# Edge network sweep of a graph kernel: expanded keys evicted ahead of head 3's norm, and VectorE's rectifier in eight pieces between the steps of the norm chain

## The chip, the cores and the metric

The kernel runs on one core of a Trainium2 chip. The metric is the device time of one execution in microseconds (us). Times before: 12400.16 us, median of 3 runs (12395.85 to 12402.57).

## What is computed

The reference is four graph layers on one graph of 6250 nodes and 206250 edges (100000 edges in both directions and a self loop for each node), 64 features a node, each layer followed by a residual sum and a layer norm: a normalised graph convolution (L0), an edge network with four heads (L1), a rectified message sum (L2), and an attention by cosine (L3). The change lies in L1 alone. What it computes for every edge and head h:

```python
alpha = concat([K_v[dst] * K_v[src], K_v[dst] * K_E], 1) * scale   # 128 values
gate  = sigmoid(layernorm(alpha) * ln_g + ln_b)
m     = (concat([V_v[src], V_E], 1) @ Wu[h] + bu[h]) * gate
m     = leaky(layernorm(m @ Wm[h] + bm[h]) * mln_g + mln_b)        # leaky: max(v, 0.01 v)
heads.append(segment_sum(m, dst, N))
```

Here `K_v = x @ Kv2v[h]`, `K_E = edge_feature @ Ke2v[h]`, and the V's alike; `K_v[dst]` are the keys that the kernel expands from nodes to edges.

## The kernel before, in words

The program has stages one behind the other: degrees, a dense adjacency matrix in HBM and the keys of the edges (to about 4160 us), the edge network's sweep, called sweep1 (4166 to 10470 us), then L2 and L3. The edges are sorted by destination and cut into tiles of 128 edges; four tiles (G = 4) make a group, and sweep1 runs over NG = 404 groups. Each engine has its own instruction stream, all written out by hand with semaphores; each runs an iteration i of a software pipeline in which the stages of several groups meet. The first 8 iterations and the last ones are written out, the rest run in a hardware loop of four iterations.

In iteration i, in this order on each engine:

- **TensorE**: `turn_x` (4 transposes of group i's features, L1233); `turn(0)`, `m_u(0)`, `turn(1)`, `m_u(1)` (`turn(h)`: 4 transposes of head h's normed alpha of group i-1, L1240; `m_u(h)`: two matmuls, L1248); `o_pair(0)` (L1253, L1259); `expand(i+1, 0)` (L1214: the one-hot of destinations times the nodes' keys, tiles 0 and 1, into PSUM bank 7); `turn(2)`, `m_u(2)`; `expand(i+1, 1)` (tiles 2 and 3 into the same bank 7, so it waits at L1212 for `q_out`, that ScalarE has taken the first half out); `turn(3)`, `m_u(3)`; `clear_sums` (L1266), `sums(0)` (L1274, waits for `msg_ready`), `o_pair(1)`, `sums(1)`. `turn(h)` waits for head h's norm (`normed`, L1237).
- **ScalarE**: `sigmoid(0)`, `sigmoid(1)` (L1020); the copy of the turned features (L1036); `norm(i-1, 2)` (four activations, L1014); `take_sums` (L1004, L1005); `norm(i-1, 3)`; `take_q(i+1, 0)` (L986: bank 7 to SBUF; it waits for `q_done`, the matmuls of `expand`, and sets `q_out`); `sigmoid(2)`; `take_o(0)` (L1027, L1028); `take_q(i+1, 1)`; `sigmoid(3)`; `norm(i, 0)`, `norm(i, 1)`, which wait for VectorE's chain; `take_o(1)`.
- **VectorE**: `stats` of tiles 0 and 1 (8 bn_stats, L716); `gate_m(0)` (L722, waits for `sigmoid(0)`); `stats` of tiles 2 and 3; `gate_m(1)`; the rectifier `leaky` of group i-4's messages y (L742, one instruction over 1024 columns, behind a wait for `y_affine`); the **chain**, 15 small steps (L761 to L788) that make the inverse roots for the alpha norm of group i and the output norm of group i-3, with a wait for the step before (`settle`, L751) between dependent ones; among them a reduction over 1040 columns (L764); `gate_m(2)`, `gate_m(3)` (waits for `sigmoid(3)`); `product` (L699); `turn_hot` (L706); and y = o times its inverse root (L800, sets `chain2`).
- **GpSimd**: four gathers (L1434), then `affine` of the y that L800 left (L1486, L1489, sets `y_affine`); it waits at L1486 for `chain2`.
- **SyncE** only issues the loads: kept keys, edge features, the nodes' keys near a group, destination rows, one-hots.

Of the kernel before, what the change touches and what calls it, by code (L numbers as in the profile page):

```python
# [20 lines left out]
ALU = mybir.AluOpType  # L21
ACT = mybir.ActivationFunctionType
AX = mybir.AxisListType.X
# [13 lines left out]
NG = T // G  # L37
# [54 lines left out]
def after(eng, semaphore, value):  # L92

    if not isinstance(value, int) or value > 0:
        eng.wait_ge(semaphore, value)


def gnn(nc, a, out):
    ctx = ExitStack()
    with ctx:  # L100
# [157 lines left out]
        o_sq = [view(G * H * (D + 1), [G * H, D + 1]) for _ in range(2)]  # L258
        y = [view(G * H * D, [G * H, D]) for _ in range(2)]
        st = view(G * H * 6, [G * H, 6])  # L260
        var, u = (view(2 * G * H, [2 * G * H]) for _ in range(2))
# [89 lines left out]
        chain1 = sem("chain1")  # L351
# [8 lines left out]
        o_taken = sem("o_taken")  # L360
# [3 lines left out]
        y_affine = sem("y_affine")  # L364
        msg_ready = sem("msg_ready")
        CH = 15
# [74 lines left out]
        def _(dve):  # L441
            V = nc.vector
# [84 lines left out]
            for c in range(EDGES):  # L527
                count(base_f, RUNS, c, whole_runs)
                if (c + 1) % PART == 0:
                    dve.wait_ge(dve_step, vcount[0])  # L530
                    part = slice(c + 1 - PART, c + 1)
# [25 lines left out]
            for j in range(1, S):  # L557
                own = col_f[:, j * R:(j + 1) * R]
# [22 lines left out]
            for i in range(3):  # L581
                part = bm_part[i][:, :].rearrange("p (h d) -> p h d", h=H)
# [72 lines left out]
            for half in range(2):  # L655
                dve.wait_ge(pe_batch, pe_number["fold0", half])
                own = acc[0:D, 0, half * HALF:(half + 1) * HALF].rearrange("p (i n) -> p i n", n=CH_N)
# [31 lines left out]
            Q = G * H  # L689
# [19 lines left out]
            def sweep1(i, k, s, inside):  # L709

                now = [inside or 0 <= i - lag < NG for lag in range(5)]
                z, odd = s % 2, (s + 1) % 2
# [24 lines left out]
                    stats(3)  # L737
                if now[1]:
                    gate_m(1)
                if now[4]:  # L740
                    dve.wait_ge(y_affine, 2 * (i - 3))
                    V.scalar_tensor_tensor(y[z], y[z], 0.01, y[z], ALU.mult, ALU.max).then_inc(msg_ready, 1)  # L742


                n = [0]

                def small_step(ins):
                    ins.then_inc(chain1, 1)
                    n[0] += 1

                def settle():  # L751
                    dve.wait_ge(chain1, i * CH + n[0])

                if now[0]:
                    dve.wait_ge(stats1, Q * (i + 1))
                if now[3]:
                    dve.wait_ge(o_taken, 2 * (i - 2))
                root = rstd[z]
                if now[2]:
                    dve.wait_ge(normed, Q * (i - 1))  # L760
                small_step(V.tensor_tensor(d2, st[:, :, 1], st[:, :, 4], ALU.subtract))  # L761
                small_step(V.tensor_tensor(sm, st[:, :, 1], st[:, :, 4], ALU.add))
                small_step(V.scalar_tensor_tensor(m2, st[:, :, 2], P * EPS1, st[:, :, 5], ALU.add, ALU.add))
                small_step(V.tensor_reduce(var[:, Q:2 * Q], o_sq[odd], AX, ALU.add))  # L764
                settle()

                small_step(V.scalar_tensor_tensor(d2, d2, P / 4.0, d2, ALU.mult, ALU.mult))
                settle()
                small_step(V.tensor_tensor(var[:, 0:Q], d2, m2, ALU.add))
                settle()  # L770
                small_step(V.tensor_scalar(root.bitcast(I32), var.bitcast(I32), -0.5, MAGIC, ALU.mult, ALU.add))

                settle()
                small_step(V.scalar_tensor_tensor(u, root, 1.0, root, ALU.mult, ALU.mult))
                settle()
                small_step(V.tensor_tensor(u, u, var, ALU.mult))
                settle()
                small_step(V.scalar_tensor_tensor(u, u, -10.0 / 3.0, u, ALU.add, ALU.mult))
                settle()
                small_step(V.scalar_tensor_tensor(root, u, 5.0, root, ALU.add, ALU.mult))  # L780
                settle()
                small_step(V.scalar_tensor_tensor(u, root, -0.5 * 0.375 ** 3 * P ** 0.5, root, ALU.mult, ALU.mult))
                settle()
                small_step(V.tensor_tensor(u, u, var, ALU.mult))
                settle()
                small_step(V.scalar_tensor_tensor(root, u, 1.5 * 0.375 * P ** 0.5, root, ALU.add, ALU.mult))
                settle()
# [151 lines left out]
        def _(act):  # L939
# [42 lines left out]
            def take_q(g, j):  # L982

                act.wait_ge(q_done, 2 * g + j + 1)
                after(act, products, g)
                A.activation(q[:, 2 * j:2 * j + 2, :].rearrange("p t n -> p (t n)"), psum[:, 7, :],  # L986
                             ACT.Copy).then_inc(q_out, 1)

            def sweep1(i, k, s, inside):
# [8 lines left out]
                def take_sums():  # L998

                    act.wait_ge(sums1, 2 * (i - 4))  # L1000
                    after(act, added1, 3 * (i - 5))
                    for half in range(2):
                        own = acc[:, half, bass.ds(held[s], 1)]
                        A.activation(own, psum[:, half, 0:1], ACT.Identity, bias=own).then_inc(added1, 1)  # L1004
                    A.activation(acc[:, :, 1:NW][:, :, bass.ds(held[s], G * WIN - 1)], psum[:, 0:2, 1:G * WIN],  # L1005
                                 ACT.Copy).then_inc(added1, 1)
# [32 lines left out]
                    norm(i - 1, (s + 3) % U, odd, 2)  # L1039
                if now[5]:  # L1040
                    take_sums()
                if now[1]:
                    norm(i - 1, (s + 3) % U, odd, 3)
                if inside or i + 1 < NG:
                    take_q(i + 1, 0)
                if now[1]:
                    sigmoid(2)
                if now[2]:
# [649 lines left out]
```

## Time and profile before

The profiled execution took 12403.94 us; its span from the first to the last instruction is 12402.1 us.

| engine | busy, us | share of the span |
|---|---|---|
| TensorE matmul | 9426.5 | 76% |
| VectorE | 8554.8 | 69% |
| ScalarE | 6685.0 | 54% |
| GpSimd | 6548.5 | 53% |

These shares are averages over stages with different limits. Sweep1 takes half of the span, from about 4160 to 10470 us, and only there do all engines run at once; the change touches only that stretch. So the views to read are those of windows inside it. The whole-span chain of waits is spread over five stages and says little about one of them.

### The profile page before, as it was taken

Reading aid. Unit: us, or ns where it says so; the run is one execution under the profiler, and the core shown is the slowest. Engines: PE = TensorE matmul, PEld = TensorE weight load, DVE = VectorE, ACT = ScalarE, POOL = GpSimd, SP = SyncE. Lnnn points to the kernel's source line nnn. Section 1 sums busy time; section 2 is a strip of 40 time slices with the busy share of each in tenths; the row PEclk is TensorE's granted clock in tenths of the full one; section 3 lists DMA queues with packets and bytes.
Section 4 is the critical chain, followed back from the end, with each engine's and each line's share of the span. In section 5 each row is a group of like instructions: output and inputs, shape, how many; then the busy total and the mean of one; then the engine's idle time right before and its main releaser. Section 6 shows DMA issues by size and latency. Waiting matters only on the chain.

```text
span 12402.1 us, 195341 instructions
## 1 busy us (share of the span) xinstructions
PE 9426.5 (76%) x48422; PEld 6119.9 (49%) x48423; DVE 8554.8 (69%) x19173; ACT 6685.0 (54%) x13488; POOL 6548.5 (53%) x4199
## 2 busy tenths in 40 slices
PE   1344444444446799999999999999999997769996
PEld 1233333333322566666666666666666665333222
DVE  4233333333311799999999999999999998047896
ACT  0111111111100488888888888888888886026442
POOL 1588888888840366666666666666666664000000
PEclk9999999999999799999999999999999998989997
DMA  9866666666678455555555555555555553869663
GB/s 412 257 163 150 152 150 151 150 152 152 149 234 337 153 152 152 152 152 152 152 152 152 152 152 152 152 152 152 152 152 152 152 152 109 355 255 358 206 218 118
DMA packets 1446102, 2253.42 MB, mean 182 GB/s; under 512 B 352561, under 2 KB 981762, under 8 KB 1432131
## 3 DMA queue, kind: packets, MB, share of 16 engines
q1 hardware_dynamic: 1129144, 1975.67, 48.0%
q0 software_dynamic: 312672, 272.36, 13.6%
q10 hardware_dynamic: 4144, 3.51, 0.1%
q8 instruction: 88, 1.44, 0.0%
q14 instruction: 54, 0.44, 0.0%
HBM read 1758.01 MB, written 492.97 MB: 181 GB/s over the span
## 4 chain that ended last, share of the span: by engine, by line
PE 42%; POOL 15%; ACT 15%; issue 12%; DMA 8%; DVE 3%; SPq 3%; ACTq 1%; DVEq 0%; POOLq 0%; PEldq 0%
POOL adj L1473 14%; ACT arena L1014 8%; PE psum L1274 6%; PE psum L1259 6%; PE psum L1248 5%; PE psum L1345 5%; DMA arena<-adj 5%; PE psum L1240 4%; PE psum L1214 4%; SPq L1520 3%; ACT acc L1005 3%; DMA adj<-put_val,put_idx 3%; PE psum L1390 2%; PE psum L1266 2%; ACT arena L986 2%
## 5 line engine op out<-in xcount | busy, mean ns | idle before, releaser
L1473 POOL DMA_INDIRECT adj<-put_val,put_idx x1616 | 2640.7, 1634 | 842.6 <-issue 477.2
L1155 PE MATMUL psum<-ke,arena 64*128 64x256 f32 x3232 | 1451.8, 640 | 1883.2 <-DMA arena<-in_edge_t 1883.2
L1014 ACT ACTIVATE arena<-arena 128x128 f32<-128x128 f32 x6464 | 2624.5, 501 | 19.1 <-DVE arena L788 9.1
L1434 POOL DMA_INDIRECT arena<-table,idx_blk x1616 | 1938.1, 1199 | 451.3 <-issue 409.3
L1155 PEld LDWEIGHTS psum<-ke,arena 64*128 64x128 f32 x3232 | 1041.6, 330 | 2292.9 <-issue 2025.9
L971 ACT ACTIVATE arena<-psum 128x512 f32<-128x512 f32 x808 | 482.5, 597 | 2921.5 <-PE psum L1155 2611.7
L1486 POOL TENSOR_TENSOR arena<-arena,mg 128x1024 f32<-128x1024 f32 x404 | 953.6, 2360 | 1973.7 <-DVE arena L800 1973.7
L1248 PE MATMUL psum<-arena,wvu 128*128 128x512 f32 x3232 | 1655.3, 594 | 0.0
L1259 PE MATMUL psum<-wm,arena 128*128 128x64 f32 x12928 | 1616.3, 278 | 0.0
L1259 PEld LDWEIGHTS psum<-wm,arena 128*128 128x128 f32 x12928 | 1505.4, 192 | 183.3 <-issue 181.5
L1020 ACT ACTIVATE arena<-psum,cols 128x512 f32<-128x512 f32 x1616 | 1263.2, 782 | 495.0 <-PE psum L1240 494.6
L614 DVE TENSOR_TENSOR arena<-arena 128x1024 f32<-128x1024 f32 x202 | 247.8, 1227 | 1723.2 <-DMA arena<-key_lin 1723.2
L716 DVE BATCH_NORM_STATS2 arena<-arena 128x6 f32<-128x128 f32 x6464 | 1320.9, 277 | 0.0
L722 DVE SCALAR_TENSOR_TENSOR arena<-psum,cols,arena 128x512 f32<-128x512 f32 x1616 | 1199.4, 746 | 24.5 <-PE psum L1248 4.5
L1214 PE MATMUL psum<-arena 128*128 128x256 f32 x3232 | 897.5, 400 | 364.4 <-ACT arena L986 315.5
L1240 PE MATMUL psum<-ident,arena 128*128 128x128 f32 x6464 | 970.8, 273 | 5.6 <-ACT arena L1014 4.4
L1489 POOL TENSOR_TENSOR arena<-arena,mb 128x1024 f32<-128x1024 f32 x404 | 952.6, 2358 | 31.7
L1240 PEld LDWEIGHTS psum<-ident,arena 128*128 128x128 f32 x6464 | 795.8, 141 | 303.7 <-issue 212.4
L1274 PE MATMUL psum<-arena 128*128 128x128 f32 x6464 | 921.2, 286 | 6.5 <-DVE arena L742 6.5
L699 DVE TENSOR_TENSOR arena<-arena 128x2048 f32<-128x2048 f32 x404 | 921.4, 2281 | 5.8 <-ACT arena L986 5.8
L1214 PEld LDWEIGHTS psum<-arena 128*128 128x128 f32 x3232 | 551.9, 191 | 742.0 <-ACT arena L986 631.8
L1274 PEld LDWEIGHTS psum<-arena 128*128 128x128 f32 x6464 | 789.1, 192 | 179.6 <-issue 179.6
(218 smaller groups left out, 12787.6 us busy)
## 6 DMA issues: line engine op xcount, KB each, us to landing
arena<-adj SPq DMA_DIRECT2D x192, 1568.0 KB, 12.5
arena<-adj SPq DMA_DIRECT2D x336, 896.0 KB, 4.7
kept_keys<-arena SPq DMA_DIRECT2D x404, 512.0 KB
arena<-kept_keys SPq DMA_DIRECT2D x404, 512.0 KB
arena<-table1q SPq DMA_DIRECT2D x1616, 128.0 KB
adj<-arena SPq DMA_DIRECT2D x98, 1568.0 KB
arena<-in_edge_t SPq DMA_DIRECT2D x808, 128.0 KB
kept_hot<-arena SPq DMA_DIRECT2D x404, 256.0 KB
```

Of the source, the lines that this page charges most:

```text
L716: V.bn_stats(st[:, t * H + h, :], halves(pair[s][:, :, D:PAIR])[:, t, :, h * D:(h + 1) * D]).then_inc(stats1, 1)
L722: V.scalar_tensor_tensor(gm[odd][:, h, :, :].rearrange("p t n -> p (t n)"), psum[:, 4 + h % 2, :], cols[:, 0, h:h + 1], gate[:, h % 2, :], ...
L1014: A.activation(to, at_, ACT.Identity, bias=shift[z][:, n:n + 1], scale=rstd[z][:, n:n + 1]).then_inc(normed, 1)
L1020: A.activation(gate[:, h % 2, :], psum[:, 2 + h % 2, :], ACT.Sigmoid, bias=cols[:, 2, h:h + 1], scale=cols[:, 1, h:h + 1]).then_inc(gated, 1)
L1155: last = M.matmul(psum[:, 2 + 2 * z + j, t * H * D:(t + 1) * H * D], edge0[z][:, 2 * j + t, :], ke[D:P, :], start=True, stop=True)
L1214: last = M.matmul(psum[:, 7, t * H * D:(t + 1) * H * D], hot_t[:, 2 * j + t, :], near[at_z][:, 2 * j + t, :], start=True, stop=True)
L1240: last = M.transpose(psum[:, 2 + h % 2, t * P:(t + 1) * P], normal[h % 2][:, t, :], ident[:, :])
L1248: M.matmul(psum[:, 4 + h % 2, :], wvu[:, h, :], xt[prev].rearrange("p t n -> p (t n)"), start=True, stop=True).then_inc(m_done, 1)
L1259: last = M.matmul(psum[:, 6, at_ + h * D:at_ + (h + 1) * D], gm[z][:, h, 2 * j + t, :], wm[:, h, :], start=False, stop=t * H + h == 2 * H - 1)
L1274: last = M.matmul(psum[:, half, bass.ds(held[G * s + t], WIN)], y[z][:, t * H + 2 * half:t * H + 2 * half + 2, :].rearrange("p h d -> p (h ...
L1434: K.indirect_dma_start(out=dst[:, t, :], out_offset=None, in_=table, in_offset=bass.IndirectOffsetOnAxis(ap=idx[:, t:t + 1], axis=0)).then ...
L1473: K.indirect_dma_start(out=adj, out_offset=bass.IndirectOffsetOnAxis(ap=put_idx[s][:, j:j + 1], axis=0), in_=put_val[s][:, j:j + 1], in_of ...
```

## The change

Two edits, both inside sweep1.

On ScalarE `take_q(i + 1, 0)` moves in front of `norm(i - 1, 3)`; the order of everything else stays.

On VectorE the rectifier L742, one instruction over 16 x 64 = 1024 columns, becomes eight instructions over 2 x 64 = 128 columns each (`leaky(0)` to `leaky(7)`). They no longer stand ahead of the chain: one stands behind each of eight steps of it, from `var[:, 0:Q]` (L769) to the second `u * var` (L784), ahead of the wait for that step. The wait for `y_affine` goes with `leaky(0)`, and `msg_ready` is set by `leaky(7)`. The reduction L764 moves from the fourth to the fifth place of the chain, behind the squared difference, with the wait for `o_taken` now just ahead of it.

```diff
--- before.py
+++ after.py
@@ -737,12 +737,19 @@
                     stats(3)
                 if now[1]:
                     gate_m(1)
-                if now[4]:
-                    dve.wait_ge(y_affine, 2 * (i - 3))
-                    V.scalar_tensor_tensor(y[z], y[z], 0.01, y[z], ALU.mult, ALU.max).then_inc(msg_ready, 1)
 
 
                 n = [0]
+                piece = Q // 8
+
+                def leaky(part):
+                    if now[4]:
+                        if part == 0:
+                            dve.wait_ge(y_affine, 2 * (i - 3))
+                        own = y[z][:, part * piece:(part + 1) * piece, :]
+                        done = V.scalar_tensor_tensor(own, own, 0.01, own, ALU.mult, ALU.max)
+                        if part == 7:
+                            done.then_inc(msg_ready, 1)
 
                 def small_step(ins):
                     ins.then_inc(chain1, 1)
@@ -753,35 +760,45 @@
 
                 if now[0]:
                     dve.wait_ge(stats1, Q * (i + 1))
-                if now[3]:
-                    dve.wait_ge(o_taken, 2 * (i - 2))
+                else:
+                    after(dve, chain1, i * CH)
                 root = rstd[z]
                 if now[2]:
                     dve.wait_ge(normed, Q * (i - 1))
                 small_step(V.tensor_tensor(d2, st[:, :, 1], st[:, :, 4], ALU.subtract))
                 small_step(V.tensor_tensor(sm, st[:, :, 1], st[:, :, 4], ALU.add))
                 small_step(V.scalar_tensor_tensor(m2, st[:, :, 2], P * EPS1, st[:, :, 5], ALU.add, ALU.add))
+                settle()
+
+                small_step(V.scalar_tensor_tensor(d2, d2, P / 4.0, d2, ALU.mult, ALU.mult))
+                if now[3]:
+                    dve.wait_ge(o_taken, 2 * (i - 2))
                 small_step(V.tensor_reduce(var[:, Q:2 * Q], o_sq[odd], AX, ALU.add))
                 settle()
-
-                small_step(V.scalar_tensor_tensor(d2, d2, P / 4.0, d2, ALU.mult, ALU.mult))
-                settle()
                 small_step(V.tensor_tensor(var[:, 0:Q], d2, m2, ALU.add))
+                leaky(0)
                 settle()
                 small_step(V.tensor_scalar(root.bitcast(I32), var.bitcast(I32), -0.5, MAGIC, ALU.mult, ALU.add))
+                leaky(1)
 
                 settle()
                 small_step(V.scalar_tensor_tensor(u, root, 1.0, root, ALU.mult, ALU.mult))
+                leaky(2)
                 settle()
                 small_step(V.tensor_tensor(u, u, var, ALU.mult))
+                leaky(3)
                 settle()
                 small_step(V.scalar_tensor_tensor(u, u, -10.0 / 3.0, u, ALU.add, ALU.mult))
+                leaky(4)
                 settle()
                 small_step(V.scalar_tensor_tensor(root, u, 5.0, root, ALU.add, ALU.mult))
+                leaky(5)
                 settle()
                 small_step(V.scalar_tensor_tensor(u, root, -0.5 * 0.375 ** 3 * P ** 0.5, root, ALU.mult, ALU.mult))
+                leaky(6)
                 settle()
                 small_step(V.tensor_tensor(u, u, var, ALU.mult))
+                leaky(7)
                 settle()
                 small_step(V.scalar_tensor_tensor(root, u, 1.5 * 0.375 * P ** 0.5, root, ALU.add, ALU.mult))
                 settle()
@@ -1039,10 +1056,10 @@
                     norm(i - 1, (s + 3) % U, odd, 2)
                 if now[5]:
                     take_sums()
+                if inside or i + 1 < NG:
+                    take_q(i + 1, 0)
                 if now[1]:
                     norm(i - 1, (s + 3) % U, odd, 3)
-                if inside or i + 1 < NG:
-                    take_q(i + 1, 0)
                 if now[1]:
                     sigmoid(2)
                 if now[2]:
```

## Rows read from the trace of the kernel before

**Rows 1.** Windows: us, busy of each engine, clock, DMA share, GB/s; sweep1.

```profile
4700.00:10500.00 5800.00, 5489.14 (x32666) 3926.01 (x32664) 5444.11 (x14463) 5092.96 (x11116) 3533.25 (x2305) 1.00 0.54 150
```

**Rows 2.** Waits, 4800 to 10400: who waited for whom, us, times, longest.

```profile
PE psum L1214 <- ACT arena L986: 282.5, 360, 0.9
...
DVE arena L742 <- POOL arena L1489: 151.2, 360, 0.5
```

**Rows 3.** Timeline, one iteration: TensorE; start, us, instructions, idle before.

```profile
7508.36 1.02 PE L1248 MATMUL psum<-arena,wvu 128*128 128x512 f32 x2
...
7509.23 0.60 PE L1240 MATMUL psum<-ident,arena 128*128 128x128 f32 x4
...
7512.77 1.08 PE L1214 MATMUL psum<-arena 128*128 128x256 f32 x4
...
7514.12 1.02 PE L1248 MATMUL psum<-arena,wvu 128*128 128x512 f32 x2
...
7515.93 1.13 PE L1214 MATMUL psum<-arena 128*128 128x256 f32 x4 [0.78 <-ACT arena L986]
...
7516.90 0.60 PE L1240 MATMUL psum<-ident,arena 128*128 128x128 f32 x4
...
7518.82 1.16 PE L1274 MATMUL psum<-arena 128*128 128x128 f32 x8
...
7524.74 0.60 PE L1240 MATMUL psum<-ident,arena 128*128 128x128 f32 x4
```

**Rows 4.** The same timeline: ScalarE, from sigmoid(1) to sigmoid(3).

```profile
7509.86 0.78 ACT L1020 ACTIVATE arena<-psum,cols 128x512 f32<-128x512 f32 x1 [0.44 <-PE psum L1240]
...
7513.75 1.65 ACT L1014 ACTIVATE arena<-arena 128x128 f32<-128x128 f32 x4
...
7515.29 0.59 ACT L986 ACTIVATE arena<-psum 128x512 f32<-128x512 f32 x1
...
7517.86 0.79 ACT L1020 ACTIVATE arena<-psum,cols 128x512 f32<-128x512 f32 x1
```

**Rows 5.** The same timeline: VectorE and GpSimd around the rectifier and chain.

```profile
7507.83 1.64 DVE L716 BATCH_NORM_STATS2 arena<-arena 128x6 f32<-128x128 f32 x8
...
7512.83 1.23 DVE L742 SCALAR_TENSOR_TENSOR arena<-arena 128x1024 f32<-128x1024 f32 x1 [0.35 <-POOL arena L1489]
...
7513.97 0.18 DVE L761 TENSOR_TENSOR arena<-arena 128x16 f32<-128x16 f32 x1
...
7515.24 0.96 POOL L1434 DMA_INDIRECT arena<-table,idx_blk  x1 [0.30 <-issue]
...
7515.73 0.17 DVE L769 TENSOR_TENSOR arena<-arena 128x16 f32<-128x16 f32 x1
...
7515.94 0.25 DVE L771 TENSOR_SCALAR arena<-arena 128x32 int32<-128x32 int32 x1
...
7517.98 1.53 DVE L722 SCALAR_TENSOR_TENSOR arena<-psum,cols,arena 128x512 f32<-128x512 f32 x2
```

**Rows 6.** Timeline of VectorE, early in the sweep.

```profile
4347.35 1.23 DVE L742 SCALAR_TENSOR_TENSOR arena<-arena 128x1024 f32<-128x1024 f32 x1 [0.51 <-POOL arena L1489]
...
4362.76 1.23 DVE L742 SCALAR_TENSOR_TENSOR arena<-arena 128x1024 f32<-128x1024 f32 x1 [0.50 <-POOL arena L1489]
```

**Rows 7.** Timeline of TensorE behind the last product: turn(3) without expand.

```profile
10418.66 0.66 PE L1240 MATMUL psum<-ident,arena 128*128 128x128 f32 x4 [1.22 <-ACT arena L1014]
```

**Rows 8.** Timeline of ScalarE there: norm(3).

```profile
10416.96 1.65 ACT L1014 ACTIVATE arena<-arena 128x128 f32<-128x128 f32 x4
```

**Rows 9.** Timeline of VectorE, end of the sweep.

```profile
10441.01 1.23 DVE L742 SCALAR_TENSOR_TENSOR arena<-arena 128x1024 f32<-128x1024 f32 x1 [4.90 <-POOL arena L1489]
```

**Rows 10.** DMA queues, 4300 to 10380: instruction packets, MB, share.

```profile
q14 instruction: 5, 0.04, 0.0%
q8 instruction: 2, 0.03, 0.0%
```

**Rows 11.** DMA issues of the whole run: KB each, us to landing.

```profile
arena<-kept_hot SPq DMA_DIRECT2D x404, 256.0 KB, 3.4
```

## The prediction

> **What bounds the kernel now.** I read three views of sweep1. First the windows: from 4700 to 10500 us TensorE is busy 5489 of 5800 us and VectorE 5444 [rows 1], at a granted clock of 1.00 (the 2.4 GHz level). Two engines at 94% mean that shares can't say which one sets the pace. Next the waits: TensorE waits at L1214 for ScalarE's L986 in all of 360 iterations, 282.5 us together, and VectorE at L742 for GpSimd's L1489, 151.2 us [rows 2]. These are the only stalls of the two that come every time. Then the timeline of one iteration: turn(1) starts at 7509.23 and again at 7524.74 [rows 3], 15.51 later (15.52 over longer stretches, which I use). Times below are in us after 7500.
>
> The loop that closes at 15.52 runs through two engines. ScalarE starts sigmoid(1) at 9.86 as turn(1) ends, and works without a gap through norm(2), take_sums and norm(3) (from 13.75) to take_q, 15.29 to 15.88 [rows 4]; only then, at 15.93, may TensorE start expand(i+1, 1), after 0.78 of idling [rows 3]. The rest, from there to the next turn(1), is TensorE's own work. The bank was full at 12.77 + 1.08 = 13.85 [rows 3], so take_q comes 1.44 late, behind a norm that TensorE doesn't need yet.
>
> A second loop is almost as long. Early in the sweep two rectifiers stand 4362.76 - 4347.35 = 15.41 apart, each behind a wait of 0.51 for GpSimd [rows 6]: L800, then affine, then L742, then all of VectorE's iteration. VectorE's own work is thus 15.41 - 0.51 = 14.90. So moving take_q alone could give only about 15.52 - 15.41 = 0.11 a group; it takes both edits to go further.
>
> **Part 1, take_q ahead of norm(3).** Nothing is added; two pieces trade places. ScalarE is free at 13.75, but the bank is full at 13.85 and a release takes about 0.04, so take_q starts at 13.89 (0.14 of new waiting) and is done at 14.48. It held the engine for 15.77 - 15.29 = 0.48 before norm(3)'s successor started (ScalarE has no gap there), so norm(3) starts at 14.37 instead of 13.75. TensorE: m_u(2) starts at 14.12 [rows 3]; an m_u that waits for nothing is followed after 9.23 - 8.36 = 0.87 [rows 3], so expand(i+1, 1) starts at 14.99, not 15.93. Its wait is gone. What is late next is turn(3), which needs norm(3). It follows expand after 16.90 - 15.93 = 0.97 [rows 3], so it could start at 15.96; behind the last product, where no expand stands between, turn(3) started at 10418.66 after a norm(3) begun at 10416.96 [rows 7, 8], 1.70 later. So 14.37 + 1.70 = 16.07 instead of 16.90: **0.83 saved**, and a remnant of 0.11 waiting at turn(3). The new period of this loop is 14.69. With norm(3) wholly hidden it would be 14.58, TensorE's own work; that is the floor. Behind turn(3) nothing else depends on the order: sigmoid(2) starts 0.14 later, as does sigmoid(3) (now 17.86, then 18.00 to 18.79) [rows 4]. The SyncE load and GpSimd gather that wait for `normed` fetch for groups two iterations ahead, so 0.6 later is covered; bare, it would cost those 0.6.
>
> **Part 2, the rectifier.** Removed from VectorE: L742, which holds it for 13.97 - 12.83 = 1.14 [rows 5], and the 0.51 wait ahead of it. The chain's first steps, with the 1.23 of the reduction, run meanwhile: L761 to L769 took 15.73 - 13.97 = 1.76 [rows 5], so leaky(0) asks for `y_affine` over 1.7 later than L742 would, and the wait is gone. If it came back, all chain steps, both gate_m and the product would queue behind it. Added: eight pieces between dependent steps. From L769 to gate_m(2) ten starts take 17.98 - 15.73 = 2.25, 0.225 each [rows 5]; that is latency, since the work is far smaller. What a piece holds: eight bn_stats of 128 columns take 1.64, at most 0.205 each, and L742 takes 1.14 for 1024 columns [rows 5], which makes 1.04 ns a column and 0.07 fixed. A 32-column step then holds 0.105, a 128-column piece 0.205, together **0.31 from step to step**, since the step's result has arrived while the piece runs. Growth of the chain: 8 x (0.31 - 0.225) = 0.68. VectorE's work: 14.90 - 1.14 + 0.68 = 14.44, under 14.69 by 0.25. Moving the reduction only reorders; its steps sum to the same 1.76, or one settle (0.1) less. Late next on VectorE is gate_m(3), which waits for sigmoid(3) at 18.79; VectorE idles its 0.25 there. The messages: leaky(7) ends about 0.7 ahead of gate_m(2), near 17.5, and sums(0) wants them at 18.82 - 0.83 = 17.99 [rows 3]. That cover is 0.4 thick.
>
> No row shows a piece between two dependent steps. Lower bound: fully inside the latency, s = 0.225, growth 0 and no effect on the time, as TensorE leads. Upper bound: nothing overlaps. L742 lasts 1.23 and holds 1.14, so a piece lasts 0.205 + 0.09 = 0.29; a 16-column step lasts 0.17 [rows 5], one of 32 columns 0.19, and the next starts 0.225 - 0.19 = 0.035 after its end: 0.19 + 0.035 + 0.29 + 0.035 = 0.55. I take 0.31, because bn_stats and L742 both overlap their neighbours [rows 5]. In general VectorE's work is 11.96 + 8s: it passes 14.69 at s = 0.341 and 15.52 at s = 0.445. GpSimd's gathers run beside the chain; L771 takes 0.25 where it ends with a gather [rows 5] against about 0.19 for its neighbours, so up to 0.06 x 4 = 0.24 a group might be added, just the slack.
>
> The Trainium skill speaks against this part ("VectorE: DVE Perf Modes", section "The DRAIN you can't avoid"): the next instruction does not start until the pipe is empty. The trace disagrees: at 0.29 each, eight bn_stats would take 2.3, and they take 1.64 [rows 5]. By that rule s would be near 0.55, and the change would lose; it is rival C.
>
> **The sum.** 404 groups less the first few, which follow other waits: 400 x 0.83 = 332. In the last three iterations VectorE waits 4.90 for GpSimd [rows 9]; there the chain's first 1.76 now runs under the wait while the pieces lengthen what follows by 0.68 and the last message waits longer, so some 4 in all. 12403.94 - 336 = 12068 for the profiled execution; the median of the runs is 3.8 lower, so **12064**. The bounds of this case: period 14.58 gives 400 x 0.94 = 376 and 12024; 14.80, with gather contention or 0.1 more at turn(3), gives 288 and 12112.
>
> **Rivals.**
> - **B, VectorE leads.** A satisfied wait lets the next step in only when the piece has ended: s = 0.105 + 0.29 + 0.035 = 0.43, work 15.40, gain 0.12 x 400 = 48, 12350; milder forms lie between this and the forecast. For: dependent steps start 0.035 after the end of the one before. Against: gate_m and stats follow each other with overlap though waits stand between them.
> - **C, slower.** The pieces and steps don't overlap at all, s = 0.55: work 16.36, 0.84 x 400 = 336 lost, 12736. It decides from s = 0.445. Against it are the 1.64 of rows 5.
> - **D, instructions fetched again.** VectorE's loop grows by 7 instructions an iteration, 28 in its body of four. Now 7 packets of instructions move in 6080 us [rows 10], so every loop stays resident. If this one no longer did, each of 98 passes would wait for a load, at most about the 3.4 of a 256 KB one-hot [rows 11], less the slack of 4 x 0.25: 98 x 2.4 = 235 given back, 12299; with a 1 us fetch, nothing. The Trainium skill ("Runtime: NRT & Kernel Launch", section "Instruction fetch mechanics") says that a branch to a page outside the two held stalls; no row of before shows such a stall.
> - **E, no effect**, if the release of bank 7 didn't gate TensorE: the wait would reappear in full at turn(3), giving 12400. Against: turn(3) has the whole expand (0.97) as cover.
>
> **How the numbers follow.** Forecast 70%; B 12%, D 8%, C 6%, E 4%. Forecast's own range is 12024 to 12112. To leave out no more than 2 in 10 the range takes in the milder halves of B and D: 12015 to 12270. A measurement of this kernel can tell about 0.2%, 25 us. Faster: forecast, D, and B nearly whole, 0.89; same 0.05; slower 0.06.
>
> **What would show it.** In the changed profile: the idle at L1214 behind ScalarE gone and about 0.1 at turn(3) in its place; turn(1) every 14.7; no wait for `y_affine`; chain steps with a piece 0.31 apart; a wait of 0.2 to 0.3 at gate_m(3) for sigmoid(3). Steps 0.35 or more apart with no idle left on VectorE mean B or C; a gap of over 1 us every fourth iteration with hundreds of instruction packets means D; idle at sums(0) would mean that the later messages bind.

## The result, and the profile of the changed kernel

The changed kernel takes 12111.44 us (median of 4, 12107.74 to 12115.86) against 12399.56 us before (median of 4, 12395.85 to 12402.57): ratio 0.9766, 95% interval [0.9755, 0.9778]. That is 288 us less where 336 were forecast, 48 us above the forecast of 12064, inside the stated range (12015 to 12270) and 0.6 us under the upper end of the forecast's own 12024 to 12112. The profiled execution took 12110.71 us, its span is 12108.9 us; against the profiled execution of before it saves 293.2 us.

In the changed file lines from the rectifier on stand 7 to 17 lower. On VectorE the pieces are L750, the chain's first steps L768, L769, L770, L773, the reduction L776, then L778 to L805, `product` L699, y's scaling L817; ScalarE has `take_q` L1003, `take_sums` L1021 and L1022, `norm` L1031, `sigmoid` L1037; TensorE `expand` L1231, `turn` L1257, `m_u` L1265, `clear_sums` L1283, `sums` L1291; GpSimd the gathers L1451 and the affine L1503, L1506.

The windows view of sweep1 (core time, busy us and instructions of TensorE, its weight loads, VectorE, ScalarE and GpSimd, clock, DMA share, GB/s) and the waits from 4800 to 10100 (us in total, times, longest):

```profile
4700.00:10200.00 5500.00, 5461.81 (x32538) 3911.58 (x32537) 5419.31 (x16989) 5062.55 (x11069) 3321.26 (x2293) 1.00 0.53 157
```

```profile
PEld psum L1257 <- ACT arena L1031: 164.8, 359, 0.5
...
PEld psum L1231 <- ACT arena L1003: 85.3, 357, 0.2
```

TensorE is now busy 5462 of 5500 us, 99.3% where it was 94.6% [rows 1]. Both stalls of [rows 2] are gone: `expand` no longer idles behind ScalarE's `take_q` (the 0.2 that is left is a weight load's), and no line of VectorE waits for GpSimd. In their place is a wait at `turn(3)` for norm(3) in each of 359 iterations, 0.46 for the weight load; TensorE's matmuls themselves lose little by it, as the timeline shows.

The timeline of one iteration (start, duration, engine and line, count, idle before):

```profile
7502.23 2.36 POOL L1506 TENSOR_TENSOR arena<-arena,mb 128x1024 f32<-128x1024 f32 x1
...
7503.68 1.08 PE L1231 MATMUL psum<-arena 128*128 128x256 f32 x4
...
7504.03 0.60 DVE L768 TENSOR_TENSOR arena<-arena 128x16 f32<-128x16 f32 x1
...
7504.56 0.17 DVE L769 TENSOR_TENSOR arena<-arena 128x16 f32<-128x16 f32 x1
...
7504.80 0.60 ACT L1003 ACTIVATE arena<-psum 128x512 f32<-128x512 f32 x1
...
7505.29 1.63 ACT L1031 ACTIVATE arena<-arena 128x128 f32<-128x128 f32 x4
...
7506.22 0.17 DVE L778 TENSOR_TENSOR arena<-arena 128x16 f32<-128x16 f32 x1
...
7506.80 0.18 DVE L785 SCALAR_TENSOR_TENSOR arena<-arena 128x32 f32<-128x32 f32 x1
...
7506.90 0.28 DVE L750 SCALAR_TENSOR_TENSOR arena<-arena 128x128 f32<-128x128 f32 x1
...
7506.98 0.66 PE L1257 MATMUL psum<-ident,arena 128*128 128x128 f32 x4
...
7507.11 0.18 DVE L788 TENSOR_TENSOR arena<-arena 128x32 f32<-128x32 f32 x1
...
7507.48 1.02 PE L1265 MATMUL psum<-arena,wvu 128*128 128x512 f32 x2
...
7508.45 0.28 DVE L750 SCALAR_TENSOR_TENSOR arena<-arena 128x128 f32<-128x128 f32 x1
...
7508.97 1.16 PE L1291 MATMUL psum<-arena 128*128 128x128 f32 x8
...
7509.04 1.54 DVE L722 SCALAR_TENSOR_TENSOR arena<-psum,cols,arena 128x512 f32<-128x512 f32 x2
...
7514.89 0.38 PE L1257 MATMUL psum<-ident,arena 128*128 128x128 f32 x2
```

turn(1) stands at 7500.14 and again at 7514.89, 14.75 later (15.51 in [rows 3]; the last line shows two of its four matmuls because the window ends there). Over 4100 us in the middle of the sweep one product follows the other after 14.784 in the mean, 15.524 before; I call this the period.

### The profile page after: what moved, and what is told of

It is laid out like the page before. It is cut to its first block, busy times and chain, and to the rows that moved or that the text cites. A ratio compares the mean times of both kernels' runs of the same rounds, so it can differ in the third digit from the quotient of the medians.

```text
span 12108.9 us, 197973 instructions
## 1 busy us (share of the span) xinstructions
PE 9428.1 (78%) x48422; PEld 6126.0 (51%) x48423; DVE 8560.2 (71%) x22001; ACT 6675.6 (55%) x13488; POOL 6342.6 (52%) x4199
## 4 chain that ended last, share of the span: by engine, by line
PE 54%; POOL 14%; DMA 10%; issue 9%; ACT 5%; SPq 3%; DVE 3%; DVEq 0%; ACTq 0%; POOLq 0%; another core or an unknown queue 0%; PEldq 0%
POOL adj L1490 14%; PE psum L1276 13%; PE psum L1265 8%; PE psum L1291 7%; PE psum L1362 5%; PE psum L1257 5%; DMA arena<-adj 5%; ACT arena L1031 5%; DMA adj<-put_val,put_idx 4%; PE psum L1231 3%; SPq L1537 3%; PE psum L1407 3%; PE psum L1270 2%; PE psum L1283 2%; PE psum L1250 1%
## 5 line engine op out<-in xcount | busy, mean ns | idle before, releaser
L1031 ACT ACTIVATE arena<-arena 128x128 f32<-128x128 f32 x6464 | 2613.6, 492 | 2.3 <-DVE arena L797 1.5
L1451 POOL DMA_INDIRECT arena<-table,idx_blk x1616 | 1726.6, 1068 | 456.5 <-issue 411.1
L1503 POOL TENSOR_TENSOR arena<-arena,mg 128x1024 f32<-128x1024 f32 x404 | 952.5, 2358 | 1889.3 <-DVE arena L817 1889.3
L1265 PE MATMUL psum<-arena,wvu 128*128 128x512 f32 x3232 | 1655.6, 594 | 0.0
L1037 ACT ACTIVATE arena<-psum,cols 128x512 f32<-128x512 f32 x1616 | 1254.8, 777 | 418.7 <-PE psum L1257 418.4
L1257 PE MATMUL psum<-ident,arena 128*128 128x128 f32 x6464 | 993.8, 276 | 28.9 <-ACT arena L1031 5.4
L1257 PEld LDWEIGHTS psum<-ident,arena 128*128 128x128 f32 x6464 | 763.4, 141 | 447.6 <-issue 212.4
L1506 POOL TENSOR_TENSOR arena<-arena,mb 128x1024 f32<-128x1024 f32 x404 | 952.5, 2358 | 31.7
L1291 PE MATMUL psum<-arena 128*128 128x128 f32 x6464 | 920.8, 286 | 8.5 <-DVE arena L750 6.3
L699 DVE TENSOR_TENSOR arena<-arena 128x2048 f32<-128x2048 f32 x404 | 921.7, 2281 | 5.8 <-issue 5.8
L750 DVE SCALAR_TENSOR_TENSOR arena<-arena 128x128 f32<-128x128 f32 x3232 | 914.7, 283 | 0.0
L1231 PE MATMUL psum<-arena 128*128 128x256 f32 x3232 | 856.0, 387 | 49.7 <-issue 47.3
L1291 PEld LDWEIGHTS psum<-arena 128*128 128x128 f32 x6464 | 790.0, 193 | 191.7 <-issue 191.7
```

The source lines that it names most:

```text
L1031: A.activation(to, at_, ACT.Identity, bias=shift[z][:, n:n + 1], scale=rstd[z][:, n:n + 1]).then_inc(normed, 1)
L1037: A.activation(gate[:, h % 2, :], psum[:, 2 + h % 2, :], ACT.Sigmoid, bias=cols[:, 2, h:h + 1], scale=cols[:, 1, h:h + 1]).then_inc(gated, 1)
L1231: last = M.matmul(psum[:, 7, t * H * D:(t + 1) * H * D], hot_t[:, 2 * j + t, :], near[at_z][:, 2 * j + t, :], start=True, stop=True)
L1257: last = M.transpose(psum[:, 2 + h % 2, t * P:(t + 1) * P], normal[h % 2][:, t, :], ident[:, :])
L1265: M.matmul(psum[:, 4 + h % 2, :], wvu[:, h, :], xt[prev].rearrange("p t n -> p (t n)"), start=True, stop=True).then_inc(m_done, 1)
L1291: last = M.matmul(psum[:, half, bass.ds(held[G * s + t], WIN)], y[z][:, t * H + 2 * half:t * H + 2 * half + 2, :].rearrange("p h d -> p (h ...
```

## The experiments

Each ratio is against the kernel before on the same chip, whose median there was 12409.46 (e1 to e4), 12400.53 (e5 to e7), 12402.54 (e8, e9) and 12404.72 us (e10).

### e1: ScalarE's swap alone

```diff
                 if now[5]:
                     take_sums()
+                if inside or i + 1 < NG:
+                    take_q(i + 1, 0)
                 if now[1]:
                     norm(i - 1, (s + 3) % U, odd, 3)
-                if inside or i + 1 < NG:
-                    take_q(i + 1, 0)
```

> Only the ScalarE edit; VectorE as before. Theory (two loops): the TensorE/ScalarE loop falls to 14.75 us, but the VectorE/GpSimd loop of 15.40 (own work 14.90 and a wait of 0.5 for the affine) then leads, so the period is 15.40, the gain 0.12 x 395 = 47, time 12350 (ratio 0.996), and the wait of 0.5 at the rectifier comes in every group. Rival (the two edits add up, each on its own stall): 0.77 a group at once, 12100, ratio 0.976.

12362.61 us, ratio 0.9964 [0.995, 0.9978], period 15.416. The waits view, 5000 to 9000:

```profile
DVE arena L742 <- POOL arena L1489: 132.1, 260, 0.5
...
PE psum L1240 <- ACT arena L1014: 106.8, 260, 0.4
```

VectorE now waits 0.51 (132.1 / 260) for GpSimd in every group where it was 0.42 (151.2 / 360, [rows 2]): with the TensorE loop shortened, the loop through L742 and the affine sets the pace, at the 15.41 that the prediction read out of [rows 6]. TensorE's surplus shows as idle at turn(3).

### e2: the pieces alone

The changed kernel with ScalarE's old order.

> Only the VectorE edit; ScalarE evicts the expanded keys behind head 3's norm as before. Theory: the TensorE/ScalarE loop stays at 15.52, time 12400 within 10 (ratio 1.000). Rival (the rectifier was what held the sweep): up to 0.7 a group gained, 12120, ratio 0.978.

12416.72 us, ratio 1.0004 [0.9995, 1.0014], period 15.540. TensorE:

```profile
7511.63 1.13 PE L1231 MATMUL psum<-arena 128*128 128x256 f32 x4 [0.80 <-issue]
```

The 0.78 of idle ahead of `expand(i+1, 1)` [rows 3] stands there undisturbed, as 0.80. e1 and e2 are worth 47 us and nothing, both together 288: two loops of nearly one length, each of which hides the other's gain.

### e3: the rectifier moved, but whole

```diff
-                        own = y[z][:, part * piece:(part + 1) * piece, :]
+                        own = y[z]
...
-                        if part == 7:
-                            done.then_inc(msg_ready, 1)
+                        done.then_inc(msg_ready, 1)
```

and only `leaky(0)` is called.

> The changed kernel with the rectifier as one instruction of 1024 columns in the place of the first piece. Theory: a step that a piece stands behind takes 0.30 instead of 0.225, so eight pieces cost 0.6 a group and one whole instruction 1.0; VectorE's loop goes from about 14.65 to 15.05 and leads; period 15.05, 0.27 x 395 = 107 slower than the changed kernel, 12218 (ratio to before 0.985). Rival (the pieces hide nothing, their fixed costs eat the gain): 12111 or less, ratio 0.977 or less.

12233.7 us, ratio 0.9857 [0.9841, 0.9873], period 15.10. VectorE and ScalarE:

```profile
7511.28 1.22 DVE L750 SCALAR_TENSOR_TENSOR arena<-arena 128x1024 f32<-128x1024 f32 x1
...
7512.42 0.17 DVE L780 TENSOR_SCALAR arena<-arena 128x32 int32<-128x32 int32 x1
...
7512.62 0.19 DVE L783 SCALAR_TENSOR_TENSOR arena<-arena 128x32 f32<-128x32 f32 x1
...
7512.85 0.19 DVE L785 TENSOR_TENSOR arena<-arena 128x32 f32<-128x32 f32 x1
...
7514.50 2.81 ACT L1023 ACTIVATE arena<-arena 128x128 f32<-128x128 f32 x7 [1.42 <-DVE arena L793]
```

The bare steps stand 0.20 to 0.23 apart, of which the step itself holds the engine for 0.105 by the prediction's estimate, and ScalarE waits 1.42 for the chain's end. So the swap and the move give 176 us, and the cutting into pieces the rest of the 288, about 112; by the periods it is 0.32 a group (15.10 less 14.78).

### e4: GpSimd's second affine instruction left out

The profile of the changed kernel has a row that the prediction did not foresee: the chain's first step, 16 columns, lasts 0.60 (L768 above; 0.599 in the median of 408), where its like lasts 0.18, and it ends 0.04 after GpSimd's L1506 (7504.63 and 7502.23 + 2.36 = 7504.59; L769 starts at 7504.56). e4 takes away what may hold it.

```diff
-                                ALU.mult).then_inc(y_affine, 1)
-                pool.wait_ge(y_affine, 2 * g + 1)
-                K.tensor_tensor(y4, y4, mb[:, :].unsqueeze(1).to_broadcast([P, G, H * D]),
-                                ALU.add).then_inc(y_affine, 1)
+                                ALU.mult).then_inc(y_affine, 2)
```

> The changed kernel without GpSimd's second affine instruction: the addition of the output norm's offset (mln_b) is left out, so messages lack it. Theory (a two-input VectorE instruction is held while a GpSimd tensor instruction runs): the chain's first step, now 0.60, lasts 0.18, since GpSimd is done 2.4 earlier; the messages come 0.4 earlier and sums(0) no longer waits; period 14.78 to 14.75, about 12098 (ratio 0.9757). Rival (the step is slow because it reads what bn_stats has just written): it stays at 0.60, time 12111.

12227.6 us, ratio 0.9852 [0.9836, 0.9868]: by the ratios 0.0086, or 107 us, slower than the changed kernel. The hold is gone, and something else has come:

```profile
7507.72 1.08 PE L1231 MATMUL psum<-arena 128*128 128x256 f32 x4
7507.75 0.95 POOL L1451 DMA_INDIRECT arena<-table,idx_blk  x1 [0.30 <-issue]
...
7508.12 0.18 DVE L768 TENSOR_TENSOR arena<-arena 128x16 f32<-128x16 f32 x1
...
7509.26 0.60 ACT L1003 ACTIVATE arena<-psum 128x512 f32<-128x512 f32 x1 [0.44 <-PE psum L1231]
...
7511.44 0.66 PE L1257 MATMUL psum<-ident,arena 128*128 128x128 f32 x4 [0.40 <-ACT arena L1031]
```

`take_q` starts 1.54 after `expand` began instead of 1.12 (7503.68 to 7504.80 above), and turn(3) 0.40 late behind it. In 203 of 332 iterations it was 1.48 or more; nearly all others kept 1.12. The theory was right on the hold (L768 is back at 0.18) and wrong on the time. GpSimd is also free 2.36 earlier, so its gathers start earlier, and e8 asks about those.

### e5: two probes on VectorE

Two more instructions of 16 columns on a scratch tile, one of one input in SBUF, one of two.

```diff
+                V.tensor_scalar(small[:, 16:32], small[:, 0:16], 2.0, None, ALU.mult)
...
+                V.tensor_tensor(small[:, 32:48], small[:, 0:16], small[:, 0:16], ALU.add)
```

> The changed kernel with two extra VectorE instructions of 16 columns an iteration on a scratch tile: one with a single SBUF input behind the first eight bn_stats, one with two SBUF inputs behind the second eight. Both stand in the time of GpSimd's affine. Theory (held while GpSimd runs): the first lasts about 0.17, the second about 1.2, to the end of the second affine instruction; the chain's first step then lasts 0.18, since the lock is over; VectorE's loop grows by gate_m(1)'s 0.65 and 0.1: period 15.4, about 12350 (ratio 0.996). Rival (the chain's first step was slow because of the bn_stats results): both probes 0.17, the first step stays at 0.60, period 14.85 to 15.0, about 12140 to 12200.

12509.61 us, ratio 1.0085 [1.0069, 1.01], period 15.79.

```profile
7506.40 2.36 POOL L1505 TENSOR_TENSOR arena<-arena,mg 128x1024 f32<-128x1024 f32 x1 [8.51 <-DVE arena L819]
...
7507.79 1.00 DVE L732 TENSOR_SCALAR small<-small 128x16 f32<-128x16 f32 x1
...
7508.83 2.36 POOL L1508 TENSOR_TENSOR arena<-arena,mb 128x1024 f32<-128x1024 f32 x1
...
7510.92 0.31 DVE L739 TENSOR_TENSOR small<-small 128x16 f32<-128x16 f32 x1
...
7511.81 0.17 DVE L770 TENSOR_TENSOR arena<-arena 128x16 f32<-128x16 f32 x1
```

The two-input probe ends at 7511.23, where L1508 ends (7511.19), and the chain's first step behind it, in the old place, is back at 0.17: held is whichever such instruction comes first, until GpSimd's instruction ends. But the one-input probe was held as well, 1.00 instead of 0.17, to 0.03 behind the end of L1505 (7508.76); I had expected it to pass freely. That is not what missed 12350: the second probe has the less left to stand, 0.31 where I expected 1.2, and the chain begins after L1508 either way. Of 259 intervals between products 227 are 15.4 to 15.5, as expected; the other 32 are 18.1 to 18.2, and in them TensorE's steps behind sums(0) last nearly twice as long. The windows view shows a granted clock of 0.97 from 5000 to 9000, where the changed kernel has 1.00. In 404 groups these breaks make some 130 of the 160 us. bn_stats and `gate_m`, which reads one operand in PSUM, run beside the affine at their usual 0.205 and 0.73.

### e6: y's scaling ahead of the product

`product` and `turn_hot` move behind the scaling of y, so that the affine starts some 2.8 us earlier, beside these two, which both have two inputs in SBUF.

```diff
-                if inside or i + 1 < NG:
-                    product(i + 1, k + (s + 1) // U, (s + 1) % U)
-                if inside or i + 2 < NG:
-                    turn_hot(i + 2)
...
+                if inside or i + 1 < NG:
+                    product(i + 1, k + (s + 1) // U, (s + 1) % U)
+                if inside or i + 2 < NG:
+                    turn_hot(i + 2)
```

> The changed kernel with the scaling of y (which releases GpSimd's affine) ahead of the product and turn_hot, two instructions with two SBUF inputs. Theory (held while GpSimd runs): they now fall into the 4.8 us of the affine and one waits for the other; period between 16 and 19, 12600 to 13800 (ratio 1.02 to 1.11). Rival (no such hold; the earlier affine only takes a wait away): period 14.75, 12098, ratio 0.976.

13148.56 us, ratio 1.0604 [1.0588, 1.062], period 17.39.

```profile
7515.26 2.29 DVE L699 TENSOR_TENSOR arena<-arena 128x2048 f32<-128x2048 f32 x1
...
7515.43 4.34 POOL L1503 TENSOR_TENSOR arena<-arena,mg 128x1024 f32<-128x1024 f32 x1 [6.01 <-DVE arena L813]
...
7517.47 2.85 DVE L706 TENSOR_TENSOR arena<-arena,rel 128x512 f32<-128x512 int32 x1
...
7519.84 2.69 POOL L1506 TENSOR_TENSOR arena<-arena,mb 128x1024 f32<-128x1024 f32 x1
```

Here is the same collision in both directions. The product was there first and keeps its 2.29; GpSimd's multiplication stands still meanwhile and takes 4.34 in place of 2.36. `turn_hot` then comes second and takes 2.85 in place of 0.68: it ends at 7520.32, 0.55 behind L1503 (7519.77). Whoever comes second stands until the first is nearly done and then takes its own whole time. The start of that time, counted back from its end, lies 0.12 to 0.15 before the recorded end of the first in every case here: `turn_hot` 7520.32 - 0.68 = 7519.64 against 7519.77, L768 7504.63 - 0.18 = 7504.45 against 7504.59, GpSimd's L1503 behind the product 7519.77 - 2.36 = 7517.41 against 7517.55.

The period is not the price of the hold alone: 118 of 235 intervals are 16.4, the rest 17.9 to 19.7, and the windows view shows a granted clock of 0.89 from 5000 to 9100.

### e7: the sums taken behind the eviction

With the hold known, I asked which engine leads in the changed kernel: TensorE behind norm(3), or VectorE.

```diff
-                if now[5]:
-                    take_sums()
-                if inside or i + 1 < NG:
-                    take_q(i + 1, 0)
                 if now[1]:
                     norm(i - 1, (s + 3) % U, odd, 3)
+                if inside or i + 1 < NG:
+                    take_q(i + 1, 0)
+                if now[5]:
+                    take_sums()
```

> The changed kernel with ScalarE's order norm(2), norm(3), take_q(0), take_sums: the norm in front again, the eviction of the sums moved behind instead. Theory: norm(3) starts at 12.56 of the iteration, take_q at 14.1, both in time for TensorE (14.99 and 15.96), so the remnant of 0.11 at turn(3) and the slow start of 0.06 go; the TensorE loop falls to 14.58 and VectorE's loop of about 14.63 to 14.65 leads, with sums(0) waiting for the last piece: 0.14 x 395 = 55 faster than the changed kernel, 12055 (ratio 0.972). Rival (VectorE already sets the pace of the changed kernel at 14.78): no change, 12111, ratio 0.977.

12083.65 us, ratio 0.9745 [0.9732, 0.9758], period 14.706: some 27 us less than the changed kernel, half of the 55 that I expected, and the fastest of the kernels that leave nothing out. Its waits, 5000 to 9000:

```profile
PEld psum L1276 <- DVE arena L722: 29.9, 132, 0.2
PE psum L1291 <- DVE arena L750: 28.4, 129, 0.3
```

No wait at turn(3) is left; TensorE waits for VectorE now, at sums(0) and o_pair(1). TensorE's loop no longer leads, VectorE's does, at 14.71 and not at the 14.63 to 14.65 that I had put, with L768 held as before (0.595 in the median). VectorE's busy share from 5000 to 9000 is 99.3%.

### e8: e4 with the gathers held back

```diff
+                after(pool, chain1, (g - 2) * CH + 4)
                 gather(pair[s][:, :, 0:ROW1], table1, idx, kv_in[s])
```

> As e4_no_second_affine (GpSimd's second affine instruction, the addition of mln_b, is left out), and GpSimd waits ahead of each group's gathers until VectorE's chain has done its fourth step, so that the gathers start where they start in the changed kernel (0.07 before the eviction) and not 2.3 earlier. The question is why the first eviction of the expanded keys started 0.44 after its release in two iterations of three of e4. Theory: the earlier gathers delay it. Then the eviction starts 0.04 after the expansion's end again, the period falls from the mean of 15.0 to 14.75, and the kernel takes 12,080 to 12,110 us. Rival: it hangs on VectorE's own earlier lead (its first step 0.42 shorter, which this kernel leaves as it is in e4). Then the eviction is late again and the time is 12,228 within 15 us.

12104.74 us, ratio 0.9759 [0.9743, 0.9775], period 14.765.

```profile
7504.72 1.08 PE L1231 MATMUL psum<-arena 128*128 128x256 f32 x4
...
7505.12 0.18 DVE L768 TENSOR_TENSOR arena<-arena 128x16 f32<-128x16 f32 x1
...
7505.84 0.60 ACT L1003 ACTIVATE arena<-psum 128x512 f32<-128x512 f32 x1
...
7506.50 0.98 POOL L1451 DMA_INDIRECT arena<-table,idx_blk  x1 [3.19 <-DVE arena L773]
...
7508.02 0.66 PE L1257 MATMUL psum<-ident,arena 128*128 128x128 f32 x4
```

The eviction is back at 1.12 behind `expand`, and so is the time (0.0093 between the ratios, 115 us). So the loss in e4 came with the earlier gathers, not with VectorE's lead. How a gather delays it is not shown: in e4 slow and fast iterations can have their gathers at the same offsets from `expand` to 0.01 us (-1.26, 0.03, 1.29, 2.54 with 1.54; -1.26, 0.03, 1.28, 2.54 with 1.12). The gathers did not come back to their old place, though: they start 0.66 behind the eviction (7506.50) and not 0.07 ahead of it, 3.0 later than in e4. With that reserve e8 against the changed kernel also prices the hold where TensorE leads: 14.784 less 14.765, 0.02 a group; the 7 us between the times are within their noise.

### e9 and e10: e7 without the hold

e9 is e7 with e4's edit, e10 is e9 with e8's.

> The order of e7_sums_behind on ScalarE (heads 2 and 3 normalised in one go, then the eviction, then the sums) with GpSimd's second affine instruction (the addition of mln_b) left out. In e7_sums_behind VectorE's loop set the period: all its instructions stand end to end and its first step is held 0.42. Theory: with nothing of GpSimd's left to hold that step VectorE's loop falls to 14.3 and TensorE's own floor of 14.58 to 14.65 is what is left: 0.05 to 0.12 less than the 14.70 of e7_sums_behind in 400 groups, 12,035 to 12,065 us. Rival: the late eviction of e4 comes back (its release is not in what this order changes); it then holds the second expansion and the time is 12,150 to 12,230.

12260.34 us, ratio 0.9879 [0.9863, 0.9896]. Both expectations missed. (The late eviction did come back in part: it starts 1.41 or more behind `expand` in 84 of 270 iterations, where 1.33 is usual in this order.) Of 272 intervals between products in mid-sweep 62 are 14.2 to 14.4 and 121 are 14.5 to 14.9, but 17 are 15.4 to 15.7, 48 are 16.1 to 16.5 and 24 about 18. In the last kind:

```profile
5152.15 1.15 PE L1291 MATMUL psum<-arena 128*128 128x128 f32 x8 [1.24 <-DVE arena L750]
...
5153.55 3.62 PE L1276 MATMUL psum<-wm,arena 128*128 128x64 f32 x16
```

TensorE idles 1.24 ahead of sums(0), and the next `o_pair` takes 3.62 in place of 2.00, at a granted clock of 0.52 from 5153.5 to 5157.2: the 1.2 GHz level. Such a break costs 3.3 in one group.

> As e9_sums_behind_no_second (order norm(2), norm(3), eviction, sums on ScalarE; GpSimd's second affine instruction, the addition of mln_b, is left out), and the gathers wait for VectorE's fourth chain step as in e8_gathers_held. e9 ran in groups of 14.2 to 14.8 broken by groups of 16.1 and 18.0, in which TensorE waited up to 1.24 ahead of the sums and then ran at half clock for some microseconds. Theory: those breaks come from the earlier gathers, as the late eviction of e4 did. Then they are gone, the period is TensorE's own floor of 14.57 to 14.65 (VectorE's loop is 14.25 without the held step), and the kernel takes 12,035 to 12,065 us. Rival: they come from the order with a shorter VectorE loop itself, whatever the gathers do. Then the groups of 16 and 18 stay and the time is 12,200 to 12,270 us.

12004.55 us, ratio 0.9677 [0.966, 0.9693], period 14.508, not one interval over 14.65 in mid-sweep. The breaks are gone as expected; the time is 30 us below the range that I gave. The window 5000 to 9000, and two lines of TensorE:

```profile
5000.00:9000.00 4000.00, 3998.94 (x24264) 2933.64 (x24263) 3942.54 (x12679) 3749.49 (x8271) 1796.35 (x1449) 1.00 0.54 163
```

```profile
7510.70 1.03 PE L1231 MATMUL psum<-arena 128*128 128x256 f32 x4
7511.56 0.60 PE L1257 MATMUL psum<-ident,arena 128*128 128x128 f32 x4
```

TensorE is busy 3998.9 of 4000: this is its own work with next to nothing waited for, 14.51 a group (sums(0) still starts 0.04 late in the mean, so 14.47 is the floor). The prediction's floor of 14.58 was 0.11 too high, since it let turn(3) start 0.97 behind `expand`, read in [rows 3] from an `expand` that had waited; behind one that hasn't it is 0.86, as the two lines show. e9's breaks, too, came with the early gathers: nothing else differs between the two. e10 against e7 is 79 us, 0.20 a group. That is what the hold costs where VectorE leads, if the late gathers cost nothing; TensorE takes over from there.

## Why the prediction was right, point by point

- **The loop through `take_q` and norm(3)** ran as forecast, to the hundredth. With the forecast's clock shifted by 9.09, so that `expand(i+1, 0)` falls together (12.77 and 7503.68), `take_q` was to start at 7504.80 and started at 7504.80, norm(3) at 7505.28 and started at 7505.29, turn(3) at 7506.98 and started at 7506.98.
- **The period, 14.69, was sized 0.09 too short**: 403 x 0.74 = 298 us where 332 were counted, 34 of the 43 that the profiled execution missed by (12110.7 for 12068). Start to start, in the means over 4100 us before and after, only five stretches of TensorE's iteration differ by more than 0.003: m_u(2) to `expand(i+1, 1)` 1.81 and 0.86, from there to turn(3) 0.97 and 1.09 (both as forecast, 0.94 and 0.11), turn(3) to m_u(3) 0.44 and 0.49, clear_sums to sums(0) 0.53 and 0.56, sums(1) to turn_x 0.950 and 0.957. The third, 0.06, is an omission: a turn that has waited lasts 0.66, not 0.60, and the m_u behind it starts 0.50 later (7506.98 to 7507.48) instead of 0.44. I had taken the start of turn(3) from [rows 7], whose duration says 0.66, and added TensorE's remaining work as it follows an unhindered turn. 14.69 + 0.06 = 14.75, which is what the two turns(1) above are apart, and near what e8 does in the mean (14.765). The bound of 14.80 was drawn for gather contention or a longer wait at turn(3), so that 14.78 lies inside it is luck.
- **Another 0.03, at sums(0), is the wait for `y_affine`, which I had called gone.** As a wait it is gone; the conflict behind it stayed. L742 had stood behind it in the kernel before, so the chain always began with GpSimd idle and its first step took 0.18 [rows 5]. Now the chain begins while L1506 runs and stands 0.42 in the engine, in no view of waits. That ate the cover at sums(0) that the prediction called 0.4 thick, and in which it had left out the 0.24 from a message to its use: the last piece ends at 7508.73, sums(0) starts at 7508.97, and in 122 of 277 iterations this comes 0.05 or more after its unhindered start. In e8, without the hold, sums(0) starts 0.53 behind clear_sums every time; e8 gains only 0.02 in all, since 0.01 more is lost elsewhere. The last 0.007, at turn_x, has no cause shown.
- **VectorE's work.** A piece costs what was forecast: L785, L788, L791 stand 0.31 and 0.30 apart with a piece between each two. The total was over-sized, 14.44 by the forecast: the growth from the variance step to gate_m(2) is 0.57 (7506.22 to 7509.04 is 2.82, before 2.25) and not 0.68; e7, where VectorE leads, runs at 14.71 with 0.42 of hold in it, so 14.29, and e9's shortest groups are 14.2 to 14.3. This covered the hold, 14.29 + 0.42 = 14.71, just under TensorE's 14.75. That is luck: had the forecast of 14.44 been exact, the hold would have made VectorE the leader at 14.86, about 30 us slower. One sign that the prediction named did not come: no wait at gate_m(3) for sigmoid(3). With the hold VectorE has no 0.2 to 0.3 to idle away.
- **The ends of the sweep.** The seventh group's sums cost a one-off stall of 2.05 and, behind it, 3.67 for an `o_pair` of 2.00 at a granted clock of 0.50, one interval of 19.05; the start of the sweep gave 10 us less than the period says, the end 1.6 more than it where 4 were counted, and the stage began 6.8 earlier, though the change touches nothing ahead of it, which is luck again. 34 + 10 + 2.4 - 6.8 is 40 of the 43; the rest lies in the stages behind.
- **The rivals.** B (a step enters only when the piece has ended, 0.43 apart) and C (0.55) fall with the 0.30. L750 starts 0.10 after L785 did, which lasts 0.18. The rule of the Trainium skill under "The DRAIN you can't avoid" ("VectorE: DVE Perf Modes"), that the next operation waits for an empty pipe, thus doesn't bind here; the section itself excepts instructions that nothing holds. D falls by the instruction queues, which moved 9 packets from 4300 to 10100, against the 7 of [rows 10]:

```profile
q8 instruction: 4, 0.07, 0.0%
q14 instruction: 5, 0.04, 0.0%
```

E falls with the result, and e2 shows that it is true of the other half of the change.

The mechanism was thus right, with a hold that the prediction did not know of, and two sizes were off in opposite directions; that TensorE and not VectorE leads held by 0.04, where the prediction had 0.25.

## What to carry to other kernels

When two loops are of nearly one length, price a change against both: either half alone gave 47 and 0 us here, together 288. A wait that disappears may have kept two engines apart; look at what now runs side by side, and compare durations of the same instruction before and after, since a held instruction shows as a long one and not as a wait. And before an engine is relieved, ask what it will start sooner: here leaving out half of GpSimd's affine cost 107 us until its gathers were held back.

## What the runs showed of the hardware

- VectorE's tensor_tensor with two inputs in SBUF, and its f32 tensor_scalar with one, stood still until 0.12 to 0.15 before the recorded end of GpSimd's tensor instruction: 16 columns took 0.60 (L768) and 1.00 (e5, one input), 512 columns 2.85 (e6); GpSimd's 2.36 became 4.34 behind a product. bn_stats, with one input in SBUF, was not held, nor was `gate_m` with one operand in PSUM. The Trainium skill ("GPSIMD Engine Reference", section "1. Specifications") states that GpSimd shares its SBUF interfaces with VectorE and names, as those in contention, VectorE instructions with two inputs in SBUF or in a 2-port mode; the trace agrees for two inputs. For the one-input f32 `tensor_scalar` of e5, the Trainium skill ("DVE: opcode table, instruction layouts, handler registers and perf-mode slots", section "7. Perf-mode slots") says that a one-source f32 operation can run in the 2-port mode, which would put it under that rule; its mode is in no row here.
- A turn behind a wait took 0.66 and not 0.60, and delayed its successor by 0.06 (changed kernel, e8). An `expand` that had waited was followed by turn(3) after 0.97, one that had not after 0.86 (before, e10).
- TensorE starts sums(0) 0.24 after the end of the VectorE instruction that it waited for, in the changed kernel (7508.73 to 7508.97) and in e9.
- Whether TensorE's clock fell behind an idle did not go by the idle's length alone. In e9 one of 1.24 was followed by 3.62 for work of 2.00, while others of up to 1.35 were followed by none; in e5 32 idles ahead of sums(0), of 0.53 to 0.74, were followed by a stretch at half clock, while others of up to 0.89 were not.
- ScalarE's eviction started 0.36 or more late in 203 of 332 iterations of e4, and in none of e8 between 5000 and 9100 us, whose only difference is that its gathers start 3.0 later. The mechanism stays open.
